# Splitting the first variance and features by batch, and reordering VectorE and GpSimd around them, in a one-core transformer layer

## What is computed

```python
params = quantum_params[token_ids]           # 36 angles a token, gathered from 8000 rows
ev = circuit_expvals(params)                 # 6 expectation values a token (rotations, CNOT ring, 3 layers)
h = ev @ post_w.T + post_b                   # 192 features
h = h + attention(layernorm(h))              # one head of 192, softmax over the 512 keys of a batch
x = layernorm(h)
gates = top_k(x @ Wg, 2)                     # 2 of 8 experts, softmax over the two scores
h = h + sum(gate * (gelu(x @ W1[e] + b1[e]) @ W2[e] + b2[e]))
```

## Time and profile before

| | |
|---|---|
| runs | 295.48, 294.88, 294.35 us; median 294.88 |
| profiled execution, first to last instruction | 294.9 us (no other time of it is given) |
| busy time | PE 211.9, PE weight loads 150.7, POOL 210.2, DVE 175.2, ACT 121.3 us |
| mean granted TensorE clock | 0.822 |
| DMA moved | 29.86 MB |

### The profile page before, as it was taken

The page is one execution under the profiler, slowest core; times in us unless marked ns, Lnnn a source line. Parts: engine busy times, 40 slices in busy tenths (PEclk is TensorE's granted clock), DMA queues, the critical chain, the costliest instruction groups (busy, mean ns, idle before and its releaser), DMA issues.

```text
span 294.9 us, 5764 instructions
## 1 busy us (share of the span) xinstructions
PE 211.9 (72%) x1552; PEld 150.7 (51%) x1552; DVE 175.2 (59%) x687; ACT 121.3 (41%) x292; POOL 210.2 (71%) x281
## 2 busy tenths in 40 slices
PE   0760699367864678977689598999999999988000
PEld 0540554122431434544356387878789989867000
DVE  5754999756899989595887757784211000842122
ACT  2002013135351331356533467667665766745000
POOL 5777786740899697877776776777777777777750
PEclk9999999655596655579855779999999999999655
DMA  7811003994000000000012221022333315997454
GB/s 166 278 18 15 1 3 118 397 328 163 2 0 0 4 9 11 13 13 17 14 22 47 60 45 26 16 85 86 100 101 89 96 67 175 370 364 234 111 222 161
DMA packets 25659, 29.86 MB, mean 101 GB/s; under 512 B 15130, under 2 KB 19473, under 8 KB 25435
## 3 DMA queue, kind: packets, MB, share of 16 engines
q1 hardware_dynamic: 19148, 21.54, 23.3%
q0 software_dynamic: 6480, 7.94, 8.8%
HBM read 14.13 MB, written 16.02 MB: 102 GB/s over the span
## 4 chain that ended last, share of the span: by engine, by line
PE 47%; DVE 21%; POOL 12%; issue 7%; ACT 7%; DMA 4%; POOLq 1%; DVEq 0%; SPq 0%; ACTq 0%
PE bank_b L2096 24%; PE bank_a L2084 6%; POOL circuit L542 5%; PE bank_b L1855 4%; PE bank_a L1862 3%; POOL shares_out L770 3%; DVE nmax L1191 3%; POOL rs L714 2%; PE bank_c L1874 2%; ACT prob L1593 2%; POOL routed L725 1%; DMA angle_stages<-shares_out 1%; PE bank_d L1958 1%; DVE circuit L883 1%; DMA shares_out<-circuit,up 1%
## 5 line engine op out<-in xcount | busy, mean ns | idle before, releaser
L770 POOL DMA_INDIRECT shares_out<-circuit,up x71 | 72.6, 1023 | 21.6 <-issue 16.5
L2096 PE MATMUL bank_b<-wide,up 128*128 x426 | 81.0, 339 | 2.8 <-ACT up L1720 1.2
L725 POOL DMA_INDIRECT routed<-rows,slot x64 | 63.3, 989 | 23.5 <-issue 18.9
L2096 PEld LDWEIGHTS bank_b<-wide,up 128*128 128x128 f32 x426 | 69.7, 194 | 9.9 <-issue 8.3
L1732 ACT ACTIVATE circuit<-bank_b,up 128x192 f32<-128x192 f32 x71 | 29.9, 421 | 25.0 <-PE bank_b L2096 23.4
L542 POOL DMA_INDIRECT circuit<-angles,ids x32 | 31.3, 978 | 10.8 <-issue 9.0
L1720 ACT ACTIVATE up<-bank_a 128x384 f32<-128x384 f32 x71 | 34.5, 489 | 6.9 <-PE bank_a L2084 6.9
L1862 PE MATMUL bank_a<-keys_t,wt 32*128 32x512 f32 x64 | 27.8, 956 | 4.7 <-DVE nmax L1191 3.0
L1855 PE MATMUL bank_b<-queries_t,keys_t 32*128 32x512 f32 x64 | 24.6, 850 | 6.2 <-ACT keys_t L1571 3.5
L1518 DVE TENSOR_TENSOR hres<-hres,prob 128x384 f32<-128x384 f32 x12 | 6.2, 559 | 37.8 <-DMA prob<-shares_out 37.7
L1191 DVE TENSOR_REDUCE nmax<-bank_a 128x2 f32<-128x1024 f32 x16 | 19.5, 1220 | 11.3 <-PE bank_a L1862 11.3
(11 more groups left out here) (433 smaller groups left out, 392.9 us busy)
## 6 DMA issues: line engine op xcount, KB each, us to landing
routed<-pad_rows SPq DMA_DIRECT2D x8, 528.0 KB, 5.2
out<-hres SPq DMA_DIRECT2D x7, 384.0 KB, 6.0
wide<-down_w SPq DMA_DIRECT2D x1, 2304.0 KB, 12.6
prob<-shares_out SPq DMA_DIRECT2D x3, 768.0 KB, 5.4
up<-up_w SPq DMA_DIRECT2D x1, 1536.0 KB
angle_stages<-shares_out SPq DMA_DIRECT2D x2, 768.0 KB, 7.0
form_p<-shares_out SPq DMA_DIRECT2D x2, 768.0 KB, 7.1
up<-routed SPq DMA_DIRECT2D x71, 16.0 KB, 1.7
```

Of the source, the lines that this page charges most:

```text
L725: pool.indirect_dma_start(out=routed, out_offset=bass.IndirectOffsetOnAxis(slot[:, b, k, j:j + 1], 0), in_=rows[:, b, k, j, :], in_offset=None
L770: pool.indirect_dma_start(out=shares_out, out_offset=bass.IndirectOffsetOnAxis(xb[:, m, DEST:DEST + 1].bitcast(I32), 0), in_=y[:, m % RESU ...
L2096: mm = pe.matmul(bank_b[:, m % 2, 0:D], hid[:, m % STEP, c * P:(c + 1) * P], wide_flat[:, bass.ds(first + c * D, D)], start=(c == 0), stop ...
```

## The change

The first layer norm is split further. The variance is computed for parts of 1, 3, 1 and 3 batches (`VARIANCE_BATCHES`), each with its scores, and the features come in parts of 1, 1, 2, 1 and 3. `variance_tiles` and `scores` are new; `form` and `variance1` take a part instead of a chunk. The angles of chunk 0 come in pieces of 12 and 4 tiles. On DVE the small score product stands ahead of the angles, the weights stand between the two angle pieces, and the two copies of the transposed weights go to ACT. On POOL the gathers are divided anew, powers stand between them, and in the routing of batch 0 one scatter instead of two stands ahead of the first power. In `pair_strings` the call of `rstd2(0)` comes earlier. On DVE batch 0's second variance and routing come ahead of parts of the second chunk's circuit, whose end and variance come after batch 1's routing.

```diff
-    ANGLE_TILES = (16, 11, 5)
+    ANGLE_TILES = (12, 4, 11, 5)
-    ANGLE_CHUNK = (0, 1, 1)
+    ANGLE_CHUNK = (0, 0, 1, 1)
     GATHERS_EARLY = 4
-    FEATURE_BATCHES = (1, 3, 1, 3)
+    GATHERS_LATER = (2, 4, 2)
+    FEATURE_BATCHES = (1, 1, 2, 1, 3)
+    VARIANCE_BATCHES = (1, 3, 1, 3)
+    VARIANCE_OF = (0, 1, 1, 2, 3)
...
+        def variance_tiles(v):
+            c = [VARIANCE_LAST[v] <= n for n in LAST].index(True)
+            first = (VARIANCE_LAST[v] - VARIANCE_BATCHES[v]) * TILES
+            return c, first, VARIANCE_LAST[v] * TILES
...
             def rstd1(p):
-                pool.wait_ge(var1_done, c + 1)
+                pool.wait_ge(var1_done, VARIANCE_OF[p] + 1)
...
-            gather_angles(COUNT[0], COUNT[0] + GATHERS_EARLY)
+            gathered = [COUNT[0] + GATHERS_EARLY + sum(GATHERS_LATER[:n]) for n in range(len(GATHERS_LATER) + 1)]
+            gather_angles(COUNT[0], gathered[0])
             join()
             constants()
+            gather_angles(gathered[0], gathered[1])
             last_string(0)
-            gather_angles(COUNT[0] + GATHERS_EARLY, ANGLE_LAST[1])
+            gather_angles(gathered[1], gathered[2])
             rstd1(0)
+            gather_angles(gathered[2], gathered[3])
             rstd1(1)
-            gather_angles(ANGLE_LAST[1], T)
+            gather_angles(gathered[3], T)
+            rstd1(2)
             pair_strings(1, lambda: rstd2(0))
...
                 if b == 0:
-                    scatter(0, 0, 0, 2)
-                    rstd1(2)
-                    scatter(0, 0, 2, TILES)
+                    scatter(0, 0, 0, 1)
                     rstd1(3)
+                    scatter(0, 0, 1, TILES)
+                    rstd1(4)
                 else:
                     scatter(b, 0)
                 if b + 1 < POWERS:
                     rstd2(b + 1)
                 scatter(b, 1)
...
+            def scores(v):
+                form(v, 0, E)
...
+            reduce_angles(0)
+            weights()
+            reduce_angles(1)
+            rotations(0)
+            first_tails(0)
             for part in circuit_parts[1:5]:
                 part(0)
             expectations(0)
-            weights()
             variance1(0)
-            form(0, 0, E)
+            scores(0)
             features(0)
+            variance1(1)
+            scores(1)
+            row_max(0, 0)
             features(1)
-            reduce_angles(1)
-            row_max(0, 0)
+            features(2)
+            reduce_angles(2)
             row_max(0, 1)
             spread_max(0)
             row_max(1, 0)
-            reduce_angles(2)
+            reduce_angles(3)
...
             spread_max(2)
             chain_link(1, 3)
+            row_max(3, 0)
+            variance2(0)
             chain_link(1, 4)
-            row_max(3, 0)
-            chain_ends(1)
...
+            route(0)
             context(1)
-            variance2(0)
-            route(0)
-            normed(0)
             row_max(3, 1)
             spread_max(3)
+            normed(0)
+            chain_ends(1)
             slots(0)
             shares(0)
-            both_ends(1)
-            variance1(1)

             context(2)
             variance2(1)
-            form(1, 0, E)
-            features(2)
             route(1)
+            both_ends(1)
+            variance1(2)
+            scores(2)
             features(3)
+            variance1(3)
             normed(1)
             slots(1)
             shares(1)
+            scores(3)
+            features(4)
             variance2(2)
             row_max(4, 0)
...
             act.activation(gelu_ahead[:, :], half_pi[:, 0:1], ACT.Sin)
+            act.wait_ge(m2t_done, 1)
+            act.copy(mt0[:, :], bank_c[:, 0:P])
+            act.copy(mt1[:, :], bank_c[0:K1, P:2 * P]).then_inc(m2t_copied, 1)
             trig(0)
+            trig(1)
...
                 keys_copy(i + 2)
-                if i == -2:
-                    trig(1)
+                if i == -1:
+                    trig(2)
```

More of the change, by code:

```diff
@@ L68, in build @@
     CHUNK_START = LAST[0:CHUNKS - 1]
-    ANGLE_TILES = (16, 11, 5)
+    ANGLE_TILES = (12, 4, 11, 5)
     ANGLE_LAST = [sum(ANGLE_TILES[:p + 1]) for p in range(len(ANGLE_TILES))]
-    ANGLE_CHUNK = (0, 1, 1)
+    ANGLE_CHUNK = (0, 0, 1, 1)
     GATHERS_EARLY = 4
-    FEATURE_BATCHES = (1, 3, 1, 3)
+    GATHERS_LATER = (2, 4, 2)
+    FEATURE_BATCHES = (1, 1, 2, 1, 3)
+    VARIANCE_BATCHES = (1, 3, 1, 3)
+    VARIANCE_OF = (0, 1, 1, 2, 3)
     FEATURE_LAST = [sum(FEATURE_BATCHES[:p + 1]) for p in range(len(FEATURE_BATCHES))]
+    VARIANCE_LAST = [sum(VARIANCE_BATCHES[:v + 1]) for v in range(len(VARIANCE_BATCHES))]
     POWERS = CHUNK_BATCHES[0] - 1
@@ L675, in pair_strings @@
                 pjoin()
+                between()
                 pool.tensor_tensor(b[:, :, :, 1], r[:, 2:6, 1].unsqueeze(2).to_broadcast([P, 4, 2, n]), b[:, :, :, 0],
@@ L694, in pair_strings @@
                 pjoin()
-                between()
                 pool.tensor_tensor(d[:, :, 0], g[:, :, 0, 0], s[:, :, 1], ALU.add)
@@ L1131, in _ @@
                               ).then_inc(m2_centered, 1)
-            reduce_angles(0)
-            rotations(0)
-            first_tails(0)
             dve.wait_ge(score_done, 1)
@@ L1137, in _ @@
                               ALU.mult).then_inc(score_spread, 1)
-            dve.wait_ge(m2t_done, 1)
-            dve.tensor_copy(mt0[:, :], bank_c[:, 0:P])
-            dve.tensor_copy(mt1[:, :], bank_c[0:K1, P:2 * P]).then_inc(m2t_copied, 1)
             def weights():
@@ L1150, in weights, with form, variance1 @@
                                       scale, None, ALU.mult).then_inc(weights_done, 1)
-            def form(c, i, m):
-                n = COUNT[c]
-                tiles = slice(TILE0[c], TILE0[c] + n)
+            def form(v, i, m):
+                c, first, last = variance_tiles(v)
+                own = slice(first - TILE0[c], last - TILE0[c])
+                n = last - first
                 step(dve.tensor_tensor(
-                    form_p[:, 0:n, i, 0:m], ev[:, tiles, 0:PU].unsqueeze(2).to_broadcast([P, n, m, PU]),
+                    form_p[:, own, i, 0:m], ev[:, first:last, 0:PU].unsqueeze(2).to_broadcast([P, n, m, PU]),
                     form_w[:, i, 0:m, 0:PU].unsqueeze(1).to_broadcast([P, n, m, PU]), ALU.mult))
                 join()
-                step(dve.tensor_reduce(form_s[:, 0:n, i, 0:m], form_p[:, 0:n, i, 0:m], AX.X, ALU.add))
+                step(dve.tensor_reduce(form_s[:, own, i, 0:m], form_p[:, own, i, 0:m], AX.X, ALU.add))
                 join()
-            def variance1(c):
-                n = COUNT[c]
-                tiles = slice(TILE0[c], TILE0[c] + n)
+            def variance1(v):
+                c, first, last = variance_tiles(v)
+                own = slice(first - TILE0[c], last - TILE0[c])
                 dve.wait_ge(ev_done, c + 1)
                 dve.wait_ge(weights_done, 3)
-                form(c, 1, PU)
-                step(dve.tensor_tensor(var1_p[:, 0:n], form_s[:, 0:n, 1, 0:PU], ev[:, tiles, 0:PU], ALU.mult))
+                form(v, 1, PU)
+                step(dve.tensor_tensor(var1_p[:, own], form_s[:, own, 1, 0:PU], ev[:, first:last, 0:PU], ALU.mult))
                 join()
-                step(dve.tensor_reduce(var1_s[:, 0:n], var1_p[:, 0:n], AX.X, ALU.add))
+                step(dve.tensor_reduce(var1_s[:, own], var1_p[:, own], AX.X, ALU.add))
                 join()
-                dve.tensor_scalar(ve1[:, 0:n], var1_s[:, 0:n], EPS, None, ALU.add).then_inc(var1_done, 1)
+                dve.tensor_scalar(ve1[:, own], var1_s[:, own], EPS, None, ALU.add).then_inc(var1_done, 1)
+            def scores(v):
+                form(v, 0, E)
             def features(p):
@@ L1645, in _ @@
                 if i == 0:
-                    trig(2)
+                    trig(3)
                 if i >= 0:
```

## The result

The changed kernel takes 303.91 us (302.64 to 305.45, four runs) against 295.04 us before (294.35 to 295.48, four runs). The recorded ratio is 1.0255 [1.0206, 1.0304], some 7.5 us; the two medians lie 8.9 us apart (1.030). Run once more, beside other kernels of this study, it gave 1.0266 [1.0211, 1.0321]. In those later sets the kernel before has medians of 296.1 to 297.3 us, so kernels are compared by their ratios to before. The ratios leave out the few runs that are marked slow. The profiled execution took 302.64 us, the fastest of its four, with a span of 300.9 us; its mean granted TensorE clock is 0.79, where before had 0.822.

What follows compares the result with a forecast made beforehand. Taken to bound: POOL's scatter stream, fed by batch 7's gates from the attention pipeline. Second chunk +6.5 us, first chunk -1.3, sum +5.2 on 294.88: 300.1 us, range 296.5 to 303.0.

Steps and rivals of the forecast that it cites:

- the first chunk's gain: Batch 1's first row maximum comes at 66.4 instead of 67.71, a gain of 1.3 us.
- What bounds the kernel: POOL's scatters end the kernel; a delay of batch 7's gates reaches the end one for one, a gain only 0.9 us.
- First chunk, start: Rotations start at 27.0, 2.6 us saved; the first variance starts at 45.6 instead of 49.83.
- its result is not among DVE's waits before, so I price this at nothing: POOL's last string, delayed 1 us by gathers moved ahead of it, costs nothing, at most 1 us.
- POOL's order holds the gain back: Power of eight columns queues behind four gathers until 59.5; DVE sits in features of batches 2 and 3 from about 55.
- Second chunk: POOL waits for batch 4's variance, DVE 4.4 us for batch 1's power; batch 4's first maximum comes 6.5 us later.
- the relief: Less collision of DVE's and POOL's products before batch 0's slots' read: 0.8 us, read at 96.8 instead of 97.61.
- The rival of a relief of 0: Collision of DVE's and POOL's products moves to routing instead of vanishing; result 300.9 us; chance 0.16.
- they agree, so 300.1: Profiled span 294.9 and median of runs 294.88 taken as equal; with +5.2 us the forecast is 300.1.
- The rival that had the clock rise after the stall: TensorE's stretch from 114 to 147 runs at 2.4 GHz, returning up to 8 us: 292.1 us; chance 0.10.
- The second wait: Rival: batch 1's power comes before DVE reaches its normalisation, hiding that wait; 295.7 us; chance 0.09.
- The stream alone: Rival: later pipeline slack swallows the late maximum and POOL's scatters alone set the end; +1.8 us, 296.7; chance 0.07.

Runs made afterwards that it cites:

- e1: Changed kernel with the second chunk's orders on VectorE and GpSimd as before, so the first chunk's part alone; 0.9992 times before [0.9953, 1.0031].
- e2: Changed kernel with the first chunk as before, so the second chunk's part alone; 1.0242 times before [1.0166, 1.0318].
- e7: Changed kernel with batch 4's variance put back into VectorE's gap and batch 1's second power early on POOL; 1.0024 times before [0.9985, 1.0063].
- e8: First chunk's part alone, with the power of eight columns ahead of POOL's last four gathers; 0.9890 times before [0.9828, 0.9952].
- e3: Changed kernel with batch 1's second power moved ahead of three scatters and the power of twelve columns on POOL; 1.0202 times before [1.0126, 1.0278].
- e11: Changed kernel with batch 1's second power moved ahead of three scatters and the twelve-column power, run again; 1.0199 times before [1.0149, 1.0249].
- e12: Changed kernel with two gathers put back behind POOL's last string; one run, 303.43 us.
- e4: Changed kernel with the power of eight columns ahead of POOL's last four gathers; 1.0146 times before [1.0072, 1.0220].

## Why the prediction was right and wrong

The sign and the mechanism were right: 0.81 stood on slower. The size was short: +5.2 us forecast, +7.5 by the ratio. On the 294.88 from which the forecast set out that is 302.4, inside the range; the median of the four runs, 303.91, lies 0.9 us beyond its upper end. The range, 296.5 to 303.0, was also narrower than the bounds of the sum, 296.1 to 303.7, which it was said to take in. The term of the sum that was mis-sized is the first chunk's gain: 1.3 us forecast, none in e1 (0.9992 [0.9953, 1.0031]). With it at nothing the sum is +6.5; e2, without the first chunk's part, gave 7.2.

**What bounds the kernel: right.** In the table the delay of batch 4's maximum reaches the first result scatter within 1 us in nearly every row (e2: 6.58 and 6.46, e7: -1.01 and -1.06, e8: -3.20 and -3.66). In the exceptions (e3: 3.46 and 6.61, e11: 3.48 and 5.37, e12: 6.08 and 7.48) the stretch from batch 5's second maximum to batch 4's context took 10.7 to 11.5 us for 9.7. The changed kernel lost as much there in its first profiled execution (11.0), but had it back between batch 5's gates and batch 7's: 19.8 us, where its second execution took 21.2 and before 21.1 (granted clocks 0.76, 0.64 and 0.73). With that the last wait moved from batch 7's routing to batch 5's in the first execution and not in the second; why that stretch was shorter, the runs don't show.

**First chunk, start: one term missed.** The rotations start at 27.09 (27.0 forecast), the variance of four tiles takes 1.40 (1.4), the powers 1.12 and 1.67 (1.3 and 1.65). But the first variance starts at 46.64, not 45.6. The step that failed is "its result is not among DVE's waits before, so I price this at nothing": the price was not a wait; VectorE's products took longer. The lead over the same instructions before was 3.57 us at 32.3 and 2.13 at the end; it went while POOL's string ran beside VectorE's products. One pair of products in the changed kernel's timeline:

```profile
41.37 0.74 DVE L896 TENSOR_TENSOR circuit<-circuit,step_m 128x128 f32<-128x128 f32 x2
```

and the same pair before, when POOL's string had ended (40.81):

```profile
43.94 0.49 DVE L883 TENSOR_TENSOR circuit<-circuit,step_m 128x128 f32<-128x128 f32 x2
```

That VectorE work with two SBUF inputs contends with GpSimd is what the Trainium skill says (GPSIMD Engine Reference, Key points); the trace agrees, with 0.74 for 0.49 us. The runs show about 0.4 of the 1.04 us to come from the string's place; the rest stays open. Even in e12 the string starts 3.0 us behind the rotations, before 1.8; starting it sooner was not tried.

**POOL's order holds the gain back: right**, with 4.61 us of waiting (4.5 forecast), and e4 shows it by taking the wait away. The gain that is left was 0.5 us in the maximum for 1.3, and none in the runs of e1.

**Second chunk: right.** e2 has it without the first part, in old times: slots' read 96.45 (96.8), batch 2's context 101.19 (100.8), batch 1's normalisation 114.42 (114.25), batch 4's maximum 119.81 (119.7), so 6.58 us late for 6.5. That it fits so well is in part luck, for two errors cancel: the relief was 1.16, not 0.8, and the context came 4.74 behind the read, not 4.0. POOL's wait was 5.87 us, where some 4 were to show. The rival of a relief of 0 falls with that, though the collision did move in part: in e2 the copy of 16 elements behind the row maximum took 1.00 us there, in the changed kernel a 32-element product 1.69, each beside POOL's product of 720 elements.

**The sum: the step "they agree, so 300.1" failed.** It set a span against a median of runs. Each execution for which both are known takes 1.7 to 1.8 us more than its span (a later execution of before: 296.66 us with a span of 294.9; changed: 302.64 with 300.9). By that the profiled execution of before was not a median one but 1.8 us slower than the median of 294.88. In spans the forecast was 300.1 against 300.9, and 0.5 of these 0.8 us were there at batch 4's maximum (118.91 for 118.4). In times the same sum would have been 301.9 against 302.64.

**What remains** lies between executions: the changed kernel's run from 301.6 to 305.7 us, those of before from 294.3 to 298.4. In its profiled execution the stretch from batch 5's second maximum to batch 4's context took 11.0 us at a clock of 0.69 (1.0 is 2.4 GHz, 0.5 is 1.2 GHz), in the other 9.6 at 0.82, and in before 9.7 at 0.82. The first of these windows:

```profile
130.60:141.70 11.10, 8.91 (x77) 5.20 (x73) 7.88 (x43) 5.76 (x13) 8.11 (x9) 0.69 0.05 12
```

Over all runs the changed kernel was granted 0.776 to 0.797, before 0.799 to 0.827. Whether the new order brings on the lower clock, or the clock is just lower in waiting, the runs don't settle; e2, as late as the changed kernel, had 0.83 in that stretch. The rival that had the clock rise after the stall has fallen: the 33 us that answer to 114 to 147 before (119.7 to 152.7 in the first execution) ran at 0.74 and 0.76 in the two executions, for 0.76 before.

**The other rivals.** The second wait was not hidden (4.09 us). The stream alone explains neither e2 nor e7, and in e3 and e11 POOL waited for gates behind its late start.

## What to carry to other kernels

Before work is moved out of a place where its engine idles, find who waits for it, and follow that engine's queue up to the next thing the first engine needs: here 1.4 us of variance, moved out of a gap, made the next batch's first maximum 6.6 us late (e2) by way of six queued instructions. Engines that release each other in written orders are to be mended together: either move alone gave 0.5 to 1.1%, both gave 2.4%. And set spans against spans and times against times.

## What the runs showed of the hardware

- TensorE's granted clock differs between executions of one program at the same place. The same 32 products for batch 4's context took 1.94 us in one execution of the changed kernel and 1.08 in the other, and between batch 1's last maximum and batch 2's first the clock was 0.88 in the changed kernel but 0.50 in e3, which is the same program up to there: 4.5 and 5.3 us.
- A power on GpSimd takes 1.00 to 1.13 us for four columns, 1.63 to 1.68 for eight and 2.27 to 2.34 for twelve. Started 0.2 us behind a VectorE product of 672 elements it took 1.57 to 1.59 for four columns and 2.85 or 2.86 for twelve; behind one of 896 elements, in before, four columns took 1.83 (the first of the two in the earlier trace rows).

The 32 products in the changed kernel's first profiled execution:

```profile
137.22 1.94 PE L1897 MATMUL bank_c<-prob,u 128*32 128x128 f32 x32
```

and in its second:

```profile
137.20 1.08 PE L1897 MATMUL bank_c<-prob,u 128*32 128x128 f32 x32
```
